# Attention with one bank for all heads' values, second buffers, and new orders on all engines

## What is computed

```python
y = _layernorm(x, ln_w, ln_b)
q, k, v = (jnp.einsum('bsd,hde->bhse', y, w) for w in (wq, wk, wv))
scores = jnp.einsum('bhse,bhte->bhst', q, k) / math.sqrt(HEAD) + causal
attn = jnp.einsum('bhst,bhte->bshe', jax.nn.softmax(scores, axis=-1), v)
x = _layernorm(x + (attn.reshape(b, s, -1) @ wo + x))
x = _layernorm(x + x @ W.T + b + x @ (up_aux @ lora_up @ lora_down @ down_aux).T)
```

## Time and profile before

| | us |
|---|---|
| median of three runs (lowest, highest) | 453.59 (452.48, 453.97) |
| the profiled execution | 452.33 |
| its span, first to last instruction | 450.4 |
| busy: PE / DVE / ACT / POOL | 413.3 / 387.2 / 335.6 / 308.0 |
| share of the span: PE / DVE / ACT / POOL | 92% / 86% / 75% / 68% |
| mean granted clock of TensorE | 0.988 |

### The profile page before, as it was taken

One profiled execution on the slowest core, in us unless ns is written; L12 is line 12 of the kernel. 1 busy time (PEld: TensorE's weight loads), 2 busy tenths in 40 slices (PEclk: granted clock), 3 DMA queues, 4 the chain that ended last, 5 costly groups with the idle time before them and its releaser, 6 DMA issues.

```text
span 450.4 us, 15504 instructions
## 1 busy us (share of the span) xinstructions
PE 413.3 (92%) x5518; PEld 334.6 (74%) x5518; DVE 387.2 (86%) x1057; ACT 335.6 (75%) x858; POOL 308.0 (68%) x392
## 2 busy tenths in 40 slices
PE   3388799999989999999999999999999999989983
PEld 2266578888778887788888888888788888777652
DVE  3989788999889898899999999999999999878554
ACT  2206677788778887888898888888888888777850
POOL 6947476777667777667777777877767777745541
PEclk9999999999999999999999999999999999999995
DMA  3564666656776666566766656666666765652111
GB/s 84 144 163 114 170 169 169 157 159 174 171 186 159 163 164 175 149 178 168 188 189 179 177 161 182 170 172 162 182 160 166 183 177 154 162 150 85 49 40 32
DMA packets 77864, 69.11 MB, mean 153 GB/s; under 512 B 9291, under 2 KB 68482, under 8 KB 77826
## 3 DMA queue, kind: packets, MB, share of 16 engines
q1 hardware_dynamic: 77250, 68.49, 57.6%
q10 hardware_dynamic: 576, 0.13, 0.1%
HBM read 47.07 MB, written 20.99 MB: 151 GB/s over the span
## 4 chain that ended last, share of the span: by engine, by line
PE 65%; DMA 12%; SPq 11%; DVE 5%; issue 4%; ACT 2%; POOL 0%; POOLq 0%; DVEq 0%; ACTq 0%
PE pv_bank L1223 15%; PE score_bank L1204 10%; PE bank L1236 9%; PE bank L1231 6%; PE max_bank L1190 5%; PE max_bank L1186 5%; PE max_bank L1191 5%; PE score_bank L1205 5%; DMA out<-y 3%; PE bank L1275 3%; SPq L302 3%; DMA kx<-k_rows 3%; SPq L307 3%; PE bank L1276 2%; DMA q_rows<-parts 2%
## 5 line engine op out<-in xcount | busy, mean ns | idle before, releaser
L909 DVE TENSOR_REDUCE rowmax<-max_bank 128x2 f32<-128x512 f32 (+1 forms) x384 | 246.7, 676 | 19.3 <-PE max_bank L1191 8.3
L545 ACT ACTIVATE probs<-score_bank 128x384 f32<-128x384 f32 x512 | 222.0, 495 | 29.1 <-PE score_bank L1205 16.5
L461 POOL TENSOR_SCALAR_AFFINE_SELECT probs<-probs 128x1024 f32<-128x1024 f32 x128 | 138.8, 1092 | 68.8 <-ACT probs L545 68.7
L1204 PE MATMUL score_bank<-qx,kx 74*128 74x256 bf16 x512 | 121.0, 273 | 5.2 <-ACT probs L545 3.4
L1205 PE MATMUL score_bank<-qx,kx 74*128 74x128 bf16 x512 | 102.2, 218 | 0.0
L1223 PE MATMUL pv_bank<-probs,v_ext 128*32 128x256 f32 (+1 forms) x2048 | 98.2, 329 | 0.0
L1190 PE MATMUL max_bank<-kx,qx 128*128 128x128 bf16 x512 | 87.9, 223 | 3.1 <-DVE rowmax L909 2.9
L1191 PE MATMUL max_bank<-kx,qx 74*128 74x128 bf16 x512 | 87.5, 222 | 0.0
L1223 PEld LDWEIGHTS pv_bank<-probs,v_ext 128*32 128x32 f32 x2048 | 56.8, 109 | 32.0 <-issue 6.5
L1190 PEld LDWEIGHTS max_bank<-kx,qx 128*128 128x128 bf16 x512 | 49.2, 99 | 15.5 <-issue 5.6
L1204 PEld LDWEIGHTS score_bank<-qx,kx 74*128 74x128 bf16 x512 | 49.7, 97 | 12.4 <-ACT probs L545 5.7
(11 more groups left out here) (92 smaller groups left out, 591.7 us busy)
## 6 DMA issues: line engine op xcount, KB each, us to landing
kx<-k_rows SPq DMA_DIRECT2D x192, 96.0 KB
qx<-q_rows SPq DMA_DIRECT2D x128, 96.0 KB
qx<-q_rows SPq DMA_DIRECT2D x64, 104.0 KB
q_rows<-parts SPq DMA_DIRECT2D x32, 192.0 KB, 2.1
k_rows<-parts SPq DMA_DIRECT2D x32, 192.0 KB, 2.4
xa<-in_x SPq DMA_DIRECT2D x32, 128.0 KB, 3.7
k_rows<-parts SPq DMA_DIRECT2D x32, 128.0 KB, 2.3
xr<-in_x SPq DMA_DIRECT2D x32, 128.0 KB, 2.4
```

What stands on the lines that cost most here:

```text
L461: pool.affine_select(out=t, in_=t, compare_op=ALU.is_ge, fill=0.0, base=0, pattern=[[0, GROUP * NB], [1, P]], channel_multiplier=-1)\
L545: act.activation(probs[:, h, 0:PW], score_bank[SCORE_BANK[h]][:, 0:PW], ACT.Exp, scale=SCALE / Q_SCALE)\
L909: dve.tensor_reduce(to, of, AX.X, ALU.max).then_inc(s_mread[unit], 1)
L1204: pe.matmul(b[:, 0:SEQ], k[0:SCORE_ROWS, i, 0:P], q[0:SCORE_ROWS, i, :], start=True, stop=True)
```

## The change

Both halves of `pv` now go into the 512 columns of `pv_bank`; there is one copy, four transposes into bank 6, one reciprocal and one division per batch. `probs`, `xr`, `y`, `q_rows` and `k_rows` have two buffers, by the parity of the batch. Therefore exp waits for `pv` of two batches ago, `store_parts` for the expansion of two batches ago, and so on; in turn `expand`, `load_xr` and `store_y` now each wait until their own transfers of the batch before have landed. The mask rows of slots 2 and 3 of `qx` and `kx` are filled by DMA from slot 0 in place of DVE. Banks 6 and 7 change users: values, transposed maxima and transposed pv now use bank 6, and x and z transposes bank 7. The orders of all five engines are new, prologue and epilogue too: the weights are loaded ahead of the first x, and POOL makes the masks first.

```diff
-        probs = sb("probs", [P, HEADS, 2 * SEQ])
-        pv_s = [sb(f"pv_s{i}", [P, SEQ]) for i in range(HALVES)]
-        rden = [sb(f"rden{i}", [P, NB, HALF]) for i in range(HALVES)]
+        probs = [sb(f"probs{i}", [P, HEADS, 2 * SEQ]) for i in range(2)]
+        pv_s = sb("pv_s", [P, HALVES * SEQ])
+        rden = sb("rden", [P, NB * HALVES, HALF])
...
             def load_xr(it, o):
-                sp.wait_ge(s_z, it.done(o - 1))
-                sp.dma_start(xr[:, :, :], rows(x, it.batch(o))).then_inc(s_xr, 16)
+                used, landed = it.done(o - 2), it.done(o - 1, 16)
+                sp.wait_ge(s_z, used)
+                alone(sp, "sp")
+                sp.wait_ge(s_xr, landed)
...
             def store_parts(it, o):
-                sp.wait_ge(s_expand[0], it.done(o - 1, EXPAND))
-                sp.wait_ge(s_expand[1], it.done(o - 1, EXPAND))
+                read = it.done(o - 2, EXPAND)
+                sp.wait_ge(s_expand[0], read)
+                sp.wait_ge(s_expand[1], read)
                 alone(sp, "sp")
                 sp.wait_ge(s_p3, it.done(o))
-                for dram, which, first, n, stored in ((q_rows, 0, 0, PARTS, s_q_stored), (k_rows, 1, 0, PARTS, s_stored),
...
             def expand(it, o):
                 if it.static:
-                    sp.wait_ge(s_zero, 17)
+                    sp.wait_ge(s_zero, 1 + 16 * 2)
                     if first_use(it, o):
-                        sp.wait_ge(s_slot[it.base + o], 2)
-                sp.wait_ge(s_score[HEADS - 1], it.done(o - RING))
+                        sp.wait_ge(s_slot[it.base + o], 2 if it.base + o < FILLED else 32)
+                scored, landed = it.done(o - RING), it.done(o - 1, EXPAND)
+                sp.wait_ge(s_score[HEADS - 1], scored)
+                alone(sp, "sp")
+                sp.wait_ge(s_expand[0], landed)
+                sp.wait_ge(s_expand[1], landed)
                 alone(sp, "sp")
                 r = it.ring(o)
-                q, k = (t.rearrange("(r h) s -> r h s", h=HEADS) for t in (q_rows, k_rows))
+                q, k = (t[it.parity(o)].rearrange("(r h) s -> r h s", h=HEADS) for t in (q_rows, k_rows))
                 for half in range(HALVES):
                     heads = slice(half * HALF, half * HALF + HALF)
                     if half == 0:
...
+            def copy_mask_rows(slot, which):
+                sp.wait_ge(s_slot[0], 2)
+                tile, a = ((qx, SCORE_ROWS), (kx, SPLIT_ROWS))[which]
+                sp.dma_start(tile[slot][a:P, :, :], tile[0][a:P, :, :]).then_inc(s_slot[slot], 16)
...
             def store_y(it, o):
-                sp.wait_ge(s_y, it.done(o))
-                sp.dma_start(rows(out, it.batch(o)), y[:, :, :]).then_inc(s_st, 16)
+                made, landed = it.done(o), it.done(o - 1, 16)
+                sp.wait_ge(s_st, landed)
+                alone(sp, "sp")
+                sp.wait_ge(s_y, made)
+                sp.dma_start(rows(out, it.batch(o)), y[it.parity(o)][:, :, :]).then_inc(s_st, 16)
...
             def step(it):
-                if it.runs(-4):
-                    load_xr(it, -4)
+                if it.runs(-2):
+                    load_max_rows(it, -2)
                 if it.runs(0):
                     expand(it, 0)
-                if it.follows(4):
-                    load_xa(it, 4)
+                if it.runs(1):
+                    store_parts(it, 1)
                 if it.runs(-7):
                     store_y(it, -7)
-                if it.runs(-1):
-                    load_max_rows(it, -1)
-                if it.runs(1):
-                    store_parts(it, 1)
+                if it.runs(-3):
+                    load_xr(it, -3)
+                if it.runs(4):
+                    load_xa(it, 4)
 
...
-                if h % GROUP == 0 and (it.static or h in (8,)):
-                    act.wait_ge(s_pv[h // GROUP], it.done(o - 1))
-                act.activation(probs[:, h, 0:PW], score_bank[SCORE_BANK[h]][:, 0:PW], ACT.Exp, scale=SCALE / Q_SCALE)\
+                if h % GROUP == 0 and (it.static or h in ()):
+                    act.wait_ge(s_pv[h // GROUP], it.done(o - 2))
+                act.activation(probs[it.parity(o)][:, h, 0:PW], score_bank[SCORE_BANK[h]][:, 0:PW], ACT.Exp, scale=SCALE / Q_SCALE)\
...
-            def copy_pv(it, o, half):
-                act.wait_ge(s_pv[2 * half + 1], it.done(o))
-                if it.static:
-                    act.wait_ge(s_ot[half], it.done(o - 1))
-                act.activation(pv_s[half][:, :], pv_bank[:, 0:SEQ], ACT.Copy).then_inc(s_pvs[half], 1)
+            def copy_pv(it, o):
+                for group in () if not it.static else range(GROUPS):
+                    act.wait_ge(s_pv[group], it.done(o))
+                if it.static:
+                    act.wait_ge(s_ot, it.done(o - 1))
+                act.activation(pv_s[:, :], pv_bank[:, :], ACT.Copy).then_inc(s_pvs, 1)
...
-            def pvT(half):
-                return (bank7, bank7)[half][:, 0:SEQ].rearrange("p (n c w) -> p n c w", n=NB, c=HALF)
-
-            def reciprocals(it, o, half):
-                dve.wait_ge(s_ot[half], it.done(o))
-                dve.reciprocal(rden[half][:, :, :], pvT(half)[:, :, :, HD]).then_inc(s_rden[half], 1)
-
-            def divide(it, o, half):
-                dve.wait_ge(s_rden[half], it.done(o))
+            pvT = pvt_bank[:, :].rearrange("p (m c w) -> p m c w", m=NB * HALVES, c=HALF)
+
+            def reciprocals(it, o):
+                dve.wait_ge(s_ot, it.done(o))
+                dve.reciprocal(rden[:, :, :], pvT[:, :, :, HD]).then_inc(s_rden, 1)
+
+            def divide(it, o):
+                dve.wait_ge(s_rden, it.done(o))
                 if it.static:
                     dve.wait_ge(s_aT, it.done(o - 1))
                 if not it.static:
                     alone(dve, "dve")
-                dve.tensor_tensor(attn[:, :, half * HALF * HD:(half + 1) * HALF * HD].rearrange("p n (c e) -> p n c e", c=HALF),
-                                  pvT(half)[:, :, :, 0:HD],
-                                  rden[half][:, :, :].rearrange("p n (c o) -> p n c o", o=1).to_broadcast([P, NB, HALF, HD]),
-                                  ALU.mult).then_inc(s_norm[half], 1)
+                dve.tensor_tensor(attn[:, :, :].rearrange("p n (h c e) -> p (n h) c e", h=HALVES, c=HALF), pvT[:, :, :, 0:HD],
+                                  rden[:, :, :].rearrange("p m (c o) -> p m c o", o=1).to_broadcast([P, NB * HALVES, HALF, HD]),
+                                  ALU.mult).then_inc(s_norm, 1)
```

More of the change, by code:

```diff
@@ L693, in step @@
                     exp(it, 0, 13)
-                    copy_pv(it, 0, 0)
+                if it.runs(4):
+                    scale_yT(it, 4)
+                if it.runs(0):
                     exp(it, 0, 14)
                     exp(it, 0, 15)
-                if it.runs(1):
-                    exp(it, 1, 0)
                 if it.runs(-1):
@@ L1208, in pv @@
             def pv(it, o, group):
-                r, sub = it.ring(o), group % 2
+                r, p, half, sub = it.ring(o), it.parity(o), group // 2, group % 2
                 pe.wait_ge(s_mask[group], it.done(o))
@@ new lines, in first @@
+                max_scores(at, 2, 10)
+                scores(at, 1, 0)
+                scores(at, 1, 1)
+                max_scores(at, 2, 11)
+                scores(at, 1, 2)
+                pv(at, 0, 1)
+                pv(at, 0, 2)
+                pv(at, 0, 3)
+                scores(at, 1, 3)
+                pe.wait_ge(s_rest, at.done(4))
+                max_transpose(at, 2)
+                max_scores(at, 3, 0)
+                scores(at, 1, 4)
+                max_scores(at, 3, 1)
@@ L1508, in step @@
+                    queries_keys(it, 4)
+                if it.runs(3):
+                    max_scores(it, 3, 0)
                 if it.runs(1):
```

896 lines of the change are left out of this document (424 added, 472 removed).

## The result

| | before | after |
|---|---|---|
| median, us (lowest, highest) | 453.45 (452.48, 453.97) | 513.4 (508.87, 519.9) |
| the profiled execution, and its span | 452.33, 450.4 | 513.04, 511.2 |
| busy: PE / DVE / ACT / POOL | 413.3 / 387.2 / 335.6 / 308.0 | 436.8 / 374.8 / 335.4 / 301.0 |
| mean granted clock | 0.988 | 0.945 |

The ratio is 1.132, with a 95% interval of 1.125 to 1.139. The executions of one kernel differ by up to 2.5%, so a few us between two medians of four say nothing. The forecast was 489 us and the range ended at 507: the sign and the mechanism hold, the size does not.

The account below looks back on a forecast made before the run. TensorE was taken to bound the kernel before, at 12.20 us a turn. Span 450.4 + 45 (ring) - 6.6 (stalls) - 2 (head) - 1 (tail) = 485.8; plus 3.2 gives 489 us, range 464 to 507.

Parts of the forecast that it names:

- the ring: Waits through five engines, from one batch's first max scores (M) to the next's: 14.1 us against 12.2 of matmuls.
- the early unit: On TensorE, a batch's first max-score unit now follows the next batch's queries and keys, a third of a batch earlier.
- the maxima's wait: SP's wait for transposed row maxima, 72.4 us in all before, was to be no longer the one ending last.
- Sum 1.65 + 3 x 0.6 + 1.44 = 4.89: SP queue, store to expansion: store, then y, xr and xa, then the maxima's transfers; 5.04 us with new waits.
- I take 5.4: From an expansion's first transfer to the start of that batch's first max scores on TensorE: 5.4 us.
- Rival (c): Slow SP queue: 6.3 us for an expansion, new waits at their upper end, 15.3 us a turn, 518 us; chance 0.05.
- The page's figure: 2.0 us fixed plus bytes over 436 GB/s: expansion 4.3 us, 13.0 us a turn, whole 464 us.
- the head: The first 71.88 us, with weights loaded ahead of x and expansions issued earlier: 2 us gained.
- the tail: The last 30.3 us, with linear(30) and its scaling moved ahead of batch 31's division: 1 us gained.
- M of batch 5 is the last with a loose road: Batch 5's first max scores start unhindered; from there 26 intervals follow, costing together 45 us.
- The stalls of the middle: TensorE's stalls between 71.88 and 420.10 us, to be removed by second buffers: all 6.6 us gained.
- The parts costed at nothing: One copy, reciprocal and division in place of two each on ScalarE and VectorE: no gain in the loop.

Follow-up runs that it names:

- SP's edit: Changed kernel with y, xr and xa issued behind the expansion in the SP queue, not between a store and its expansion: 468.57 us, ratio 1.041.
- the clock's return: Changed kernel with 14 unused matmuls of 128 columns before each loop turn's first unit of max scores, filling TensorE's wait: 515.62 us, ratio 1.134.
- the run with three buffers: Kernel before with second buffers for probs, xr and y alone, its own orders and single scratch rows kept: 448.25 us, ratio 0.991.
- cutting it at VectorE: Changed kernel with VectorE's subtraction that makes rest put ahead of the row maximum of unit 0: 499.68 us, ratio 1.104.
- at ScalarE too: Changed kernel with VectorE's subtraction ahead of the row maximum and ScalarE's second-parts copy ahead of head 1's exponential: 496.59 us, ratio 1.093.

## Why the prediction was right and where it failed

**What bound the kernel before** was read rightly: with the ring opened, TensorE is again busy 350 of 358 us.

**The ring** is shown, not only argued: SP's edit opens it, the clock's return does not, transfers between store and expansion cost nothing that can be told without the early unit, and each cut at another engine brought the next strand to light. One reading on the way was wrong: before, queries and keys stood 16.0 us ahead of their max scores, which is 1.3 turns and not "nearly two". That SP stands at the store, that the maxima's wait goes, that TensorE waits before the four-matmul unit, its share of 85%, and some 30 us from batch 31's transposes to the end (29.6 measured) all came as said.

**The step that failed** is the size of the ring. Two of its terms were mis-sized. "Sum 1.65 + 3 x 0.6 + 1.44 = 4.89", with "0 to 0.5 us, I take 0.15" for the new waits, gave 5.04; it measured 5.60. The calm turns are 5.18, the turn in which the loop begins anew 5.7, the first pass about 6.3. The other is "I take 5.4" for an expansion, read from three places, of which I set the slow one aside; it measured 5.65, with 5.04 to 6.88. In a kernel with slack the slow cases are hidden, and the calm row is the price; in a ring every one is paid, and the mean is the price. For the first term the rows were in the trace of before: slow issues (104.87 and 177.55 above), and a store to expansion of 2.96 or 2.97 us wherever a pass of the loop begins (batches 16, 20 and 24), 2.2 to 2.3 in the other turns from 17 to 28. For the second, the mean of all three places, 5.21, 5.61 and 6.34, is 5.72, close to what was measured; but the spread now lay behind the issues and not in them, as the windows of batches 23 and 24 show. Rival (c), a slow queue with a ring of 15.3 and 518 us, had 0.05; the measured 14.92 lies nearer to it than to the forecast. It was no matter of one slow state of the queue but of the spread, and the range, cut at 507, left it out.

**The page's figure**: the prediction weighed the Trainium skill's "DMA: Bandwidth & Descriptors", by which an expansion would land in 4.3 us and the ring be 13.0. Between batches 8 and 28 TensorE never started on an expansion in under 5.04 us. The traces of this SP queue disagree with that estimate, as the rows before had.

**The sum.** The span was missed by 25.4 us: 16.3 in the ring's terms, 1.8 in the head (0.2 gained where 2 were taken; the step without a row), 0.3 in the tail, and 7 in the middle outside of the 20 turns. These lie in two turns: the one from batch 3's to batch 4's transposes took 17.51 us, 5.3 over 12.2, and the last one 14.02, 1.8 over. "M of batch 5 is the last with a loose road" was wrong. TensorE waited 2.45 us at that M (85.06), in the first of these turns, where with SP's edit it waited 0.83, and its clock fell behind the wait (0.93 over the turn; busy 15.06 us, 13.94 with SP's edit). With SP's edit the two turns are 14.77 and 14.03. What is left of them goes with their matmul records, 194 and 211 where a turn of the loop has 176: work that the new prologue and epilogue put between those transposes. "The change leaves every matmul and every column as it is" holds for the count, 5518 in both, and not for the place.

**The stalls of the middle** (6.6 us, "I take all of it, because every listed wait has its buffer") were worth 1.7 us in the run with three buffers. That a wait is listed does not make it late for the engine that binds: of ScalarE's 15.8 us at y's store and 11.9 for pv at most the 3.4 us reached TensorE for which it waited for exp. And a wait that goes uncovers the next, here z and an expansion. In the sum this error was hidden under the ring.

**The parts costed at nothing** (one copy, one division) were worth nothing that can be measured. The Trainium skill's advice in "Trainium Kernel Development and Optimization", Best Practices, to double-buffer is borne out by the run with three buffers, 0.9% faster, and only as far as something waits: the second scratch rows went with an order that put more between store and load, and their effect alone was not run.

## What to carry to other kernels

When a change moves a consumer forward on one engine and puts transfers between a store and its load on another, follow one batch through all queues back to where it started, and compare the round with the busy engine's turn. If the round is longer, price its steps by their means with the slow cases in, not by the calm rows: there is no slack left that hides them. And cut it where a queue stands idle anyway. Here three transfers moved by one place in the SP queue gave back three quarters of the loss, while cutting it at VectorE (14 us), and at ScalarE too (17 us), led to the next strand each time.

## What the runs showed of the hardware

- TensorE's granted clock fell to 0.50 (1.2 GHz) for 4.8 us after it had stood still for 3.65 us, in the middle of a loop at 1.00. From batch 4 on it fell behind each of the nine waits of 1.98 to 3.65 us before an M, and behind one of 1.67 us (112.86); behind another of 1.67 us (158.98), one of 1.90 and six of 1.27 to 1.54 it stayed at 1.00. On a path that is bound elsewhere this cost little: by the estimate above some 5 of 60 us.
- One issue of the SP queue is 0.37 to 0.42 us, and now and then 0.9 to 2.1 us, mostly in the first 215 us of a run (one of the kernel before stood at 422.15, 1.36 us).
- Six transfers of 96 to 104 KB issued back to back on the SP queue, with six more behind them, let TensorE start 5.04 to 6.88 us after the first issue, 5.65 on average, though their issues took 2.36 to 2.57 us each time.
- Fourteen bf16 matmuls of 128 columns that need nothing of each other took 0.94 us, first start to last end.
